# Three key tiles ahead: a new order of scores, projections and stores in an adaptive attention block

## The reference

```python
att = softmax(x, -1) / sqrt(1024); adj = s * cond[:, None, :] * att; adj[diag] = -inf
x = x + (1.0 at the top 10240 of adj per batch)
scale, shift = split(cond @ W_emb + b_emb)
xn = rms_norm(x, g_norm) * (1 + scale) + shift
q, k, v = heads(xn @ W_qkv)
q, k = rms_norm(q, g_q), rms_norm(k, g_k)
attn = softmax(q @ k.T * 64 ** -0.5)
o = attn @ v
x = x + o + o @ W_out
```

## Time and profile before

| | us |
|---|---|
| median of 3 runs (3756.02 to 3767.08) | 3757.48 |
| the profiled execution, its own time | 3765.85 |
| its span from first to last instruction | 3763.9 |
| PE busy in the span | 3484.9 |
| DVE busy | 2480.7 |
| POOL busy | 2480.0 |
| ACT busy | 2027.0 |

### The profile page before, as it was taken

How to read it: one execution, slowest core, us unless ns; L and a number is a source line. 1 busy time by engine, 2 the same in 40 slices (tenths; PEclk the granted TensorE clock), 3 DMA queues, 4 the chain that set the end, 5 groups by cost and what they waited for, 6 DMA issues and landing times.

```text
span 3763.9 us, 46982 instructions
## 1 busy us (share of the span) xinstructions
PE 3484.9 (93%) x16661; PEld 2542.8 (68%) x16672; DVE 2480.7 (66%) x4056; ACT 2027.0 (54%) x3331; POOL 2480.0 (66%) x2583
## 2 busy tenths in 40 slices
PE   4847999999999999999999999999999999999999
PEld 1225777777756677777756677777755677777754
DVE  8995777777787777777787677777777333333321
ACT  4635555555546355655545455555554455555650
POOL 2027778777646677777756677777765577777750
PEclk9966999999999999999999999999999999999999
DMA  7033223232245222222237222222235322222222
GB/s 291 1 101 112 93 98 105 99 105 101 95 154 193 95 87 99 102 96 84 73 111 235 90 85 89 85 85 88 101 110 172 112 88 87 90 84 91 77 86 94
DMA packets 163305, 399.51 MB, mean 106 GB/s; under 512 B 11848, under 2 KB 83584, under 8 KB 153216
## 3 DMA queue, kind: packets, MB, share of 16 engines
q1 hardware_dynamic: 163072, 396.52, 29.8%
HBM read 302.10 MB, written 94.37 MB: 105 GB/s over the span
## 4 chain that ended last, share of the span: by engine, by line
PE 69%; DVE 13%; POOL 10%; ACT 4%; DMA 2%; issue 2%; SPq 0%; POOLq 0%; DVEq 0%; ACTq 0%
PE pax L1467 26%; PE pst L1524 9%; PE ppv L1544 9%; PE pst L1440 8%; PE pax L1504 5%; PE ppv L1550 4%; POOL pl L530 3%; DVE mx L1225 3%; PE pst L1304 2%; PE pax L1485 2%; DMA xl<-xl_scr 2%; POOL xlo L554 1%; DVE xr L1056 1%; POOL wl L523 1%; POOL rs L618 1%
## 5 line engine op out<-in xcount | busy, mean ns | idle before, releaser
L530 POOL TENSOR_TENSOR pl<-pf,ph 128x1024 fp32r<-128x1024 f32 x512 | 1219.6, 2392 | 203.1 <-ACT pf L864 200.8
L1004 DVE TENSOR_SCALAR_CACHE_REDUCE trash<-keys,state 128x2048 uint8<-128x2048 f32 x384 | 899.2, 2342 | 7.7
L1225 DVE TENSOR_REDUCE mx<-pax 128x1 f32<-128x512 f32 x960 | 618.2, 686 | 271.2 <-PE pax L1504 270.5
L858 ACT ACTIVATE ph<-pst 128x1024 fp32r<-128x1024 f32 x512 | 523.1, 1022 | 223.3 <-PE pst L1524 215.5
L864 ACT ACTIVATE pf<-pst 128x1024 f32<-128x1024 f32 x512 | 522.7, 1021 | 0.4 <-DMA out_x<-pf 0.4
L1208 DVE TENSOR_REDUCE ss<-sq 128x4 f32<-128x256 f32 x256 | 107.3, 419 | 609.3 <-ACT sq L825 609.3
L618 POOL TENSOR_TENSOR rs<-rs,half 128x4 f32<-128x4 f32 x256 | 265.2, 1036 | 292.9 <-DVE rs L1211 288.9
L1467 PE MATMUL pax<-wh,xh 128*128 128x384 f32 x1920 | 394.2, 348 | 46.1 <-DVE vl L1218 39.8
L1467 PEld LDWEIGHTS pax<-wh,xh 128*128 128x128 f32 x1920 | 339.0, 192 | 81.4 <-DVE vl L1218 55.7
L1467 PE MATMUL pax<-wl,xh 128*128 128x384 f32 x1920 | 385.1, 339 | 0.0
L1504 PE MATMUL pax<-sA 65*128 65x512 f32 x960 | 351.7, 433 | 33.8 <-DVE mx L1225 17.5
(11 more groups left out here) (198 smaller groups left out, 5625.7 us busy)
## 6 DMA issues: line engine op xcount, KB each, us to landing
xl<-xl_scr SPq DMA_DIRECT2D x224, 512.0 KB, 3.3
wh<-w_scr SPq DMA_DIRECT2D x24, 1536.0 KB, 6.2
wl<-w_scr SPq DMA_DIRECT2D x24, 1536.0 KB, 9.6
keys<-in_x SPq DMA_DIRECT2D x32, 512.0 KB, 5.3
xl_scr<-xlo SPq DMA_DIRECT2D x64, 256.0 KB, 3.2
wo<-wo_scr SPq DMA_DIRECT2D x4, 4096.0 KB, 13.6
pf<-out_x SPq DMA_DIRECT2D x64, 256.0 KB, 3.8
out_x<-pf SPq DMA_DIRECT2D x64, 256.0 KB, 3.1
```

The costliest lines, as they stand in the source:

```text
L530: e.tensor_tensor(pl[:, w % 3, :], pf[:, w % 3, :], ph[:, w % 3, :].bitcast(F32), ALU.subtract).then_inc(t_lo, 1)
L858: e.activation(ph[:, w % 3, :], src, ACT.Exp, scale=DH ** -0.5).then_inc(t_eh, 1)
L1004: e.tensor_scalar(trash[:], kv, thr_f, None, ALU.is_ge, ALU.add, accum_out=cnt[:, c:c + 1]).then_inc(z_cnt, 1)
L1225: e.tensor_reduce(mx2[:, j // T, j % T, c:c + 1], max_banks(alone, j)[:, c, :], axis=AX, op=ALU.max).then_inc(m_mx, 1)
```

## The change

Six edits.

1. In prep pairs `Tensor.pair` issues the scores of tile t+3 (not t+2) ahead of the values of tile t. Around tile 0 the projection of token tile 1 moves ahead of the values of tile 0, and the scores of tile 3 with it; each later transpose moves from behind a projection to ahead of the next scores, which leaves it where it was between its neighbours.
2. `slots` gives 11 of the 16 row maxima to tiles 8 to 12 and 5 to tiles 13 to 15, which have no scores ahead of them any more (before: 12 to tiles 8 to 13, 4 to tiles 14 and 15).
3. ACT and POOL follow: exponentials and `low` come one token tile earlier, and ACT copies the second half of `out_rows` behind the exponentials of tile 3.
4. `Sync.pair` issues the first two `xl` loads of a pair ahead of `keep_w`, not behind it.
5. DVE's `search_update` in pairs moves behind `value_low`.
6. In `search_alone` the masks are added in 256 columns (18 matmuls for 9), DVE reduces 256 columns, and the shift of `bit` and the wait on it are gone.

The diff, without the DVE lines that only follow edit 6:

```diff
@@ Sync.load_second, Sync.pair
                 self.full_w(1)
-                self.keep_w(1)
...
             if prep:
                 for t in range(2):
                     self.load_xl(gp + 1, t)
+                if gp + 1 < PAIRS:
+                    self.keep_w(gp + 1)
             if not first:
...
                     self.full_w(gp + 2)
-                    self.keep_w(gp + 2)
@@ Pool.pair
             for t in range(2, T):
+                self.low(gp, (t + 1) // T, (t + 1) % T)
                 if prep:
                     self.prep_tile(gp + 1, t, 1 - par, False)
-                self.low(gp, (t + 1) // T, (t + 1) % T)
@@ Scalar.pair
             self.exp(gp, 0, 2, new)
+            if prep:
+                self.prep_tile(gp + 1, 1 - par, 1)
+                self.exp(gp, 0, 3)
             if not first:
                 self.out_rows(gp - 1, 1)
-            if prep:
-                self.prep_tile(gp + 1, 1 - par, 1)
-            self.exp(gp, 0, 3)
+            if not prep:
+                self.exp(gp, 0, 3)
...
             for t in range(2, T - 1):
+                self.exp(gp, (t + 2) // T, (t + 2) % T)
                 if prep:
                     self.prep_tile(gp + 1, 1 - par, t + 1, z=before[t + 1])
-                    if t < T - 2:
-                        self.stack_tile(gp + 1, 1 - par, t)
-                self.exp(gp, (t + 2) // T, (t + 2) % T)
+                    self.stack_tile(gp + 1, 1 - par, t)
...
             if prep:
-                self.stack_tile(gp + 1, 1 - par, T - 2)
+                self.exp(gp, 1, 1)
             self.out_move(gp, 0, (PAIRS - 1) * b + i)
@@ Vector.search_alone, Vector.pair
-                e.tensor_scalar(bit[:], bit[:], 1, None, ALU.logical_shift_right).then_inc(y_up, 1)
-                e.tensor_copy(ahead[:, :, 0], state[:, 0:2])
-                e.wait_ge(y_up, n + 1)
-                e.tensor_tensor(ahead[:, :, 1], state[:, 0:2], bit[:].broadcast_to([P, 2]),
+                e.tensor_copy(ahead[:, :, 0], state[:, 0:2]).then_inc(y_up, 1)
+                e.tensor_scalar(ahead[:, :, 1], state[:, 0:2], 1 << (30 - z) if z < STEPS - 1 else 0, None,
                                 ALU.bitwise_or).then_inc(y_up, 1)
...
-                e.tensor_reduce(tot[:], pst[:, 0, :], axis=AX, op=ALU.add).then_inc(y_up, 1)
+                e.tensor_reduce(tot[:], pst[:, 0, 0:WIDE], axis=AX, op=ALU.add).then_inc(y_up, 1)
...
+                if prep:
+                    self.value_low(gp + 1, 1 - par, t)
                 if t > 0 and before[t] is not None:
                     self.search_update(before[t])
-                if prep:
-                    self.value_low(gp + 1, 1 - par, t)
@@ Tensor.search_alone
-                for j in range(cuts[-1] // HALF):
+                for j in range(cuts[-1] // WIDE):
...
-                    i = e.matmul(pst[:, 0, :], ones[:, 0:P], mask[:, j * HALF:(j + 1) * HALF], start=(j == 0),
+                    i = e.matmul(pst[:, 0, 0:WIDE], ones[:, 0:P], mask[:, j * WIDE:(j + 1) * WIDE], start=(j == 0),
@@ Tensor.pair
-            slots = {8: [None, 0, 1], 9: [2, 3, None], 10: [4, 5, None], 11: [6, 7, None], 12: [8, 9, None],
-                     13: [10, 11, None], 14: [12, 13, "row"], 15: [14, 15, None]} if prep else {}
+            slots = {8: [None, 0, 1], 9: [2, 3, None], 10: [4, 5, 6], 11: [7, 8, None], 12: [9, 10, None],
+                     13: [11, 12, None], 14: [13, 14, "row"], 15: [15, None, None]} if prep else {}
+            ahead = 3 if prep else 2
...
-                if t + 2 < 2 * T and not (prep and t == 1):
-                    self.scores(gp, par, (t + 2) // T, (t + 2) % T)
+                if prep and t == 0:
+                    self.scores(gp, par, 0, 2)
+                    self.prep_tile(gp + 1, 1)
+                if prep and 0 < t < T - 1:
+                    self.transpose_tile(gp + 1, t)
+                if t + ahead < 2 * T:
+                    self.scores(gp, par, (t + ahead) // T, (t + ahead) % T)
...
                 if prep and t == 0:
-                    self.prep_tile(gp + 1, 1)
-                    self.scores(gp, par, 0, 3)
                     self.prep_tile(gp + 1, 2, hi=8)
...
-                if prep and t == 1:
-                    self.transpose_tile(gp + 1, 1)
                 if prep and 1 <= t <= T - 3:
                     self.prep_tile(gp + 1, t + 2, z=before[t + 2])
-                    self.transpose_tile(gp + 1, t + 1)
```

More of the change, by code:

```diff
@@ L58, in cond_block @@
     WARM = 8
+    WIDE = 256
     SHARE = 7 * (N // 2)
@@ L919, in pair @@
                 self.stack_tile(gp + 1, 1 - par, T - 1)
-            self.exp(gp, 1, 1)
+            else:
+                self.exp(gp, 1, 1)
             for t in range(T, 2 * T - 2):
@@ L994, in search_init @@
             if alone:
-                e.memset(bit[:], SIGN)
                 e.memset(cand, SIGN)
@@ L1300, in search_alone @@
                 alone, cuts = z in (0, STEPS), cuts_of(z)[1:]
-                for j in range(cuts[-1] // HALF):
-                    c = sum(j * HALF >= cut for cut in cuts)
+                for j in range(cuts[-1] // WIDE):
+                    c = sum(j * WIDE >= cut for cut in cuts)
                     e.wait_ge(y_mask, masks_before(z) + c + 1)
-                    i = e.matmul(pst[:, 0, :], ones[:, 0:P], mask[:, j * HALF:(j + 1) * HALF], start=(j == 0),
-                                 stop=(alone and j == cuts[-1] // HALF - 1), skip_group_check=True)
+                    i = e.matmul(pst[:, 0, 0:WIDE], ones[:, 0:P], mask[:, j * WIDE:(j + 1) * WIDE], start=(j == 0),
+                                 stop=(alone and j == cuts[-1] // WIDE - 1), skip_group_check=True)
                 if not alone:
```

## The result

The changed kernel takes **3860.57 us** (median of six runs, 3850.53 to 3869.69), the kernel before 3763.35 (six runs): a ratio of 1.0257 [1.0234, 1.0281], 97 us slower. Forecast were 3835 us and a range from 3750 to 3875: the measured time is 26 us above the forecast and 14 under the edge. The profiled execution has a span of 3850.6 us.

What follows compares the result with a forecast made beforehand. PE, busy 93% of the span, was taken as the bound, with 0.6 us to win from earlier scores. Terms -9 -17 -15 -6 -5 +51 +26 +53 = +78 on 3757.5 gave 3835 us, range 3750 to 3875.

Steps and rivals of the forecast that it cites:

- Search, -9: Search of batch 0: reducing 256 columns, not 512, saves 0.27 us in each of 33 reductions, -9 us.
- Stores behind, -17: Batch 0: first xl loads go ahead of stores, removing six waits (10.6 us) and four lower-clock costs of 1.6 us.
- `value_low`, -15: Token tile 3, searching batches: scores put ahead and update moved behind remove 21 waits, 0.7 us each, -15 us.
- POOL's `low` -6: POOL's low runs one tile earlier, removing most of 7.9 us of waits, -6 us; sign: its waits under 3 us.
- first pairs -5: First pair of a batch: the 1.78 us wait at token tile 2 may go in three pairs, 0 to -9, taken as -5.
- Token tile 2 keeps its wait: Token tile 2: DVE's L1211 comes 0.08 us after POOL's second low begins, so PE's 0.86 us wait stays.
- The late load, +51 and +26: Token tile 2's xl load, held by ACT's later copy: 24 stalls of 2.1 us, +51; lower clock afterwards, +26.
- The maxima, +53: Row maxima table: two more narrow places in each of 28 pairs, 0.95 us each, +53 us; 112 waits.
- (a): Rival: copy to ostg in time, load lands before PE asks, only maxima cost; +1, 3759 us, chance 0.13.
- (c): Rival: late load and maxima costs both absent, removed waits alone count; -52 us, 3706 us, chance 0.12.
- (b): Rival: xl load is late but maxima are free, DVE's lead being kept; +25, 3783 us, chance 0.10.
- (d): Rival: after each late load the clock stays low for a whole token tile; above 3880 us, chance 0.03.

Runs made afterwards that it cites:

- experiment 8: Changed kernel with tile 2's xl load ahead of the stores, second half two tiles ahead with old table, tile 7's transpose behind tile 10's scores: 3720.59 us, 0.9884.
- 12: Kernel before with only xl loads ahead of keep_w, search_update behind value_low, and the 256-column search: 3723.16 us, 0.9897.
- fifth experiment: Kernel before with only the search change (masks added in 256 columns, 18 matmuls a step): 3755.4 us, 0.9974.
- sixth experiment: Kernel before with only the first xl loads issued ahead of the stores of kept weights: 3750.7 us, 0.9961.
- experiment 9: Kernel before with only the new slots table of row maxima, scores still two tiles ahead: 3785.7 us, 1.0061.
- second experiment: Changed kernel with scores two tiles ahead again from tile 7 on and the old table of maxima: 3831.5 us, 1.0182.
- eleventh: Changed kernel with only the old slots table of row maxima put back, scores still three ahead: 3842.9 us, 1.0204.
- experiments 5 to 7: Kernel before with one edit each: 256-column search 0.9974, xl loads ahead of the weight stores 0.9961, value_low ahead of search_update 0.9965.
- experiment 10: Kernel before with only ACT's second out_rows copy moved behind its tile 1 copies and tile 3 exponentials: 3858.7 us, 1.0253.
- experiment 1: Changed kernel with the xl load of token tile 2 issued ahead of the ostg stores: 3754.6 us, 0.9978.

## Why the prediction was right, step by step

It was right in its mechanism, sign and places; the size of the main cost was too small. By its own steps:

- **What bounds the kernel.** That scores had 0.6 us to win was the reading that carried the rest. The row says 0.5 us after the change, and experiments 8 and 12 confirm it.
- **Search, -9.** The step is 65.25 - 60.56 = 4.69 us, the reduction 0.42 us; alone it is worth 9.5 us. The 18 narrower matmuls cost nothing that a step shows; the estimated 0.02 us of the Trainium skill (TensorE: Matmul & The Clock Gate, Back-to-back issue gap) is too small to be seen here.
- **Stores behind, -17.** 14 us alone. The wait went whole; the clock term rests on chance, for in the fifth experiment's trace, with the same stalls as before, two of six were followed by the lower clock, where the earlier trace rows and their like had four. By its interval the sixth experiment does not show that the clock gave anything back.
- **`value_low`, -15.** 12 us alone, with 12.6 us of idle time less. I gave the change two reasons for it (the scores between, the update behind); the second is enough.
- **POOL's `low` -6, first pairs -5.** Its waits fell from 7.9 to 5.1 us, so -3, and the sign that I had named, under 3 us, did not come. The row was misread: only 12 of the 21 waits, 2.8 us, are in prep pairs; the other nine lie in the last pair of each batch, which the change leaves alone. Nor was POOL's order needed, since the new table alone takes the 12 away (experiment 9). In the changed kernel no wait for `value_low` is over 0.9 us any more, so the 1.8 us waits of the first pairs are gone, as taken; but in each of the four a wait of 0.8 us for POOL's `stage` has come up at the next transpose, which the sum did not have.
- **Token tile 2 keeps its wait.** I had L1211 lose to POOL's second `low` by 0.08 us. It lost by about 0.01: that `low` begins halfway through 4.72 us from 3230.99, at 3233.35, and L1211 at 3233.36, where the earlier trace rows had them apart. PE's wait is 0.85 us, forecast 0.86.
- **The late load, +51 and +26.** The chain came out in its order and nearly in its times: the third part of token tile 2 was due 13.57 us behind the scores in the working and 13.70 us in the trace, the copy ended at +11.5 us, forecast +11.6. Mis-sized was the landing: 3.7 us from the earlier trace rows, where here 3.97 us go by until PE starts (3237.62 to 3241.59). Over the 24 pairs this load takes 3.7 to 5.2 us, 4.2 in the mean; the same load of the kernel before takes 3.4 to 4.3, 3.7 in the mean. So the mean stall is 2.51 us and not 2.1, 60 us in all, and the longest is 3.4 where the bound was 2.7. Why the load takes longer here was not tried. The clock took 33 us, since 20 of 24 stalls were followed by it and not two in three. That share is in part chance: with stalls as long, it was 15 of 24 in the second experiment's trace and 18 of 24 in the eleventh's. Together 93 for 77; the experiments say 95 to 106.
- **The maxima, +53.** 112 waits, as forecast. The first place costs 25 us, or 0.9 us a pair as the earlier trace rows say; the second 18: +43. Why the second is cheaper is not shown, and the intervals allow that it is not.

The errors partly cancel: -36 (experiments 5 to 7), -8 for POOL's `low` and the first pairs (the 5 of the latter not measured by themselves), +95 (experiment 10), +43 gives +94, and +97 was measured, where the sum had +78. Counted from the changed kernel down, the load gives 106 us back (experiment 1) and the second half with its cover 34 more (experiment 8), which leaves a kernel 44 us faster than the one before. **The step that was too small is the price of the stall**, in its length and its clock, by 18 to 29 us; the maxima were 10 to 19 too dear, and the gains 8 too large. That these errors have opposite signs is luck. Of the rivals, (a) and (c) needed the load in time, and it was late in all 24 pairs; (b) falls with experiment 9. Of (d) there was a trace: the clock cost 2.8 us behind three of the stalls and 1.45 behind seventeen.

## What to carry to other kernels

When an order on one engine is changed, follow what every moved instruction releases, through the queue that issues transfers: here a copy of 0.6 us moved behind two exponentials, and the load behind its store came late: 95 us. Issue a load that has no need of a store ahead of that store's wait. Before giving a producer more lead, read how long its consumer waits for it now: 0.6 us was all that a third tile of scores could win, and it takes the cover from the end of the loop. And when a cost is taken away, look at what it covered, for half of its price may come back as the next wait.

## What the runs showed that I had not expected

- **The lower clock came behind the longer stalls, not in proportion to them.** Stalls of PE with a mean of 1.12 us (0.29 to 2.60) were followed by slow matmuls in 2 of 24 cases, stalls of 1.92 to 3.44 us in 20 of 24 (15 and 18 of 24 in two other kernels with such stalls), stalls of 1.7 to 2.1 us in four of six in the kernel before and in two of six in the fifth experiment's run of the same place. Each costs some 1.45 us, now and then 2.8, so halving these stalls gave back twice what the waits promised (73 us for 33). What separates two stalls of one length isn't known: in the kernel before there are two of 1.68 us, one with a granted clock of 0.76 until the next projection and one with 1.00.
- **A DVE instruction on 128x4 elements took 2.39 us** in the timeline of the changed kernel, where 0.17 us is usual; of its 256 executions 27 took over 1 us, against 4 in the kernel before. It was issued as POOL went from one `low` to the next, and stayed to the end of the second (3230.99 + 4.72 = 3235.71 against 3235.75). The Trainium skill (SBUF — State Buffer, SBUF: two separate sides) has the two engines share a port pair: whichever starts first holds it for its whole instruction, and the other is blocked. The trace agrees, and shows the waiting time booked as the waiting instruction's own, so that no list of DVE's waits names it.
- **Idle time taken away is not time gained, in either direction**: 26 us of waits for POOL gave 11 us (experiment 8), while 0.33 us of idle time at a narrow place stands for 0.9 us.
